# A decoder layer on one core: four of eight scatter DMAs of a group move on GpSimd, and the third state sum moves on TensorE

## Time and profile before

| | us |
|---|---|
| median of three runs | 1041.16 |
| lowest and highest run | 1039.62, 1041.73 |
| the profiled execution, its own time | 1038.75 |
| its span, first to last instruction | 1037.0 |
| TensorE busy | 905.6 (87%) |
| ScalarE busy | 725.6 (70%) |
| VectorE busy | 711.7 (69%) |
| GpSimd busy | 581.8 (56%) |
| mean granted TensorE clock | 0.962 of 2.4 GHz |

### The profile page before, as it was taken

One profiled execution on the slowest core, in us unless ns is written; L12 is line 12 of the kernel. 1 busy time (PEld: TensorE's weight loads), 2 busy tenths in 40 slices (PEclk: granted clock), 3 DMA queues, 4 the chain that ended last, 5 costly groups with the idle time before them and its releaser, 6 DMA issues.

```text
span 1037.0 us, 29540 instructions
## 1 busy us (share of the span) xinstructions
PE 905.6 (87%) x10235; PEld 579.7 (56%) x10236; DVE 711.7 (69%) x1456; ACT 725.6 (70%) x2225; POOL 581.8 (56%) x387
## 2 busy tenths in 40 slices
PE   6699899999899798989989977986955999999997
PEld 2344554554355355435534543543435999999982
DVE  1487688787678777767867767797654666666647
ACT  3587997886798698679858865964733555555556
POOL 2598268459729945972894497288033334444420
PEclk9899999999999999999999988998976999999999
DMA  4526105200700430070043006002132111111144
GB/s 122 114 52 144 32 3 115 60 11 14 164 12 21 93 84 11 15 163 12 21 97 71 11 15 143 2 20 100 67 111 60 47 48 48 46 48 47 47 120 154
DMA packets 68475, 66.63 MB, mean 64 GB/s; under 512 B 8912, under 2 KB 62352, under 8 KB 67984
## 3 DMA queue, kind: packets, MB, share of 16 engines
q1 hardware_dynamic: 63440, 55.58, 21.7%
q0 software_dynamic: 4352, 8.99, 2.6%
q10 hardware_dynamic: 576, 0.62, 0.2%
HBM read 49.03 MB, written 16.13 MB: 63 GB/s over the span
## 4 chain that ended last, share of the span: by engine, by line
PE 45%; issue 20%; POOL 13%; ACT 10%; DVE 10%; DMA 2%; SPq 0%; POOLq 0%; DVEq 0%; ACTq 0%
PE pair_a L1702 6%; PE pair_b L1706 6%; ACT prob L696 6%; POOL xg L530 4%; POOL prob L498 4%; PE y_ps L1422 3%; PE bank L1714 3%; PE y_ps L1714 3%; PE pair_b L1502 3%; PE y_ps L1502 2%; PE bank L1513 2%; POOL hst L498 2%; DVE prob L934 2%; PE pair_a L1534 2%; PE bank L1326 1%
## 5 line engine op out<-in xcount | busy, mean ns | idle before, releaser
L655 ACT ACTIVATE decays<-w,a_neg 128x256 f32<-128x256 f32 x512 | 220.9, 511 | 48.8 <-DVE prob L934 27.1
L498 POOL TENSOR_TENSOR hst<-hst,c_rep 128x1024 f32<-128x1024 f32 x64 | 151.4, 2372 | 16.5 <-DVE hst L934 15.7
L569 POOL DMA_INDIRECT y<-aoT,dest x72 | 81.3, 1129 | 132.2 <-DVE aoT L1248 128.6
L498 POOL TENSOR_TENSOR prob<-prob,c_rep 128x1024 f32<-128x1024 f32 x56 | 132.4, 2369 | 6.6 <-DVE prob L934 5.7
L530 POOL DMA_INDIRECT xg<-x_all,pos x64 | 65.6, 1025 | 92.0 <-DVE pos L1084 80.8
L934 DVE TENSOR_TENSOR_SCAN prob<-decays,pair_b 128x1024 f32<-128x1024 f32 x32 | 73.1, 2285 | 46.8 <-issue 27.6
L1422 PE MATMUL y_ps<-hst,sum 128*32 128x256 f32 x512 | 71.6, 429 | 30.4 <-POOL prob L498 30.4
L696 ACT ACTIVATE prob<-pair_b,nmax 128x128 f32<-128x128 f32 x256 | 90.4, 401 | 5.0 <-DVE nmax L992 5.0
L696 ACT ACTIVATE prob<-y_ps,nmax 128x128 f32<-128x128 f32 x256 | 90.8, 415 | 0.0
L490 POOL TENSOR_TENSOR w<-diag,b_tok 128x1024 f32<-128x1024 f32 x32 | 61.7, 1959 | 46.7 <-DVE prob L939 23.3
L1702 PE MATMUL pair_a<-qk,u 128*128 128x128 f32 x592 | 79.1, 277 | 0.0
(11 more groups left out here) (287 smaller groups left out, 2154.2 us busy)
## 6 DMA issues: line engine op xcount, KB each, us to landing
w<-d_dram SPq DMA_DIRECT2D x64, 256.0 KB, 7.0
c_rep<-c_dram SPq DMA_DIRECT2D x64, 128.0 KB, 4.0
qk<-xg SPq DMA_DIRECT2D x79, 65.0 KB
d_dram<-zpos SPq DMA_DIRECT2D x8, 512.0 KB, 3.2
xn<-in_x SPq DMA_DIRECT2D x8, 256.0 KB, 3.1
cn<-in_ctx SPq DMA_DIRECT2D x8, 256.0 KB, 3.4
mask_b<-in_mask SPq DMA_DIRECT2D x8, 256.0 KB, 3.2
w<-in_w1T SPq DMA_DIRECT2D x1, 2048.0 KB, 7.6
```

Of the source, the lines that this page charges most:

```text
L498: g_.tensor_tensor(by_state(ring(k)), by_state(ring(k)), c_rep[:, :, toks[r]].rearrange("p q (i t) -> p i q t", i=2), ALU.mult).then_inc(s ...
L569: pool.indirect_dma_start(y2[:, :], bass.IndirectOffsetOnAxis(ap=dest[:, b:b + 1], axis=0), ys[:, b % 4, :], None).then_inc(s[f"y_out{b % ...
L655: last = A(by_state(decays[:, k % 2, :])[:, :, q, :], delta_rep[:, b, toks[r]].rearrange("p (i t) -> p i t", i=2), ACT.Exp, scale=a_neg[:, ...
```

## The change

In GpSimd's block four of the eight scatters of group m-2 stay before the products of units 0 to 3; the other four go, one each, behind the first and the second `diagonals`, behind `add_q` and behind `add_bo`. In TensorE's block sum 2 moves from `k == 13` to `k == 14`, so that it stands behind `res(c, 1)` and `entries(m, 15)`, and `x1_t(g, 0)` moves up to stand directly before it. In ScalarE's block `res_out(c, 1)` and `x1_in(g, 0)` go ahead of the first `own_k`, and the four `own_k` stand together. Nothing that is computed changes.

```diff
@@ GpSimd
                 for k in range(NU - 1):
-                    if m >= 2 and k < 2 * S:
+                    if m >= 2 and k < S:
                         scatter(m - 2, (k,))
                     times_c(m, k)
...
                 if e is not None:
                     at(pool, "hc_last", m + 1)
                     diagonals(e, 0)
+                if m >= 2:
+                    scatter(m - 2, (S,))
+                if e is not None:
                     diagonals(e, 1)
+                if m >= 2:
+                    scatter(m - 2, (S + 1,))
                 add_q(m, 1)
+                if m >= 2:
+                    scatter(m - 2, (S + 2,))
                 add_bo(m)
+                if m >= 2:
+                    scatter(m - 2, (S + 3,))
@@ ScalarE
-                own_k(g, 0)
-                own_k(g, 1)
                 if c is not None:
                     res_out(c, 1)
-                own_k(g, 2)
                 x1_in(g, 0)
-                own_k(g, 3)
+                for j in range(4):
+                    own_k(g, j)
@@ TensorE
                     if k + 1 < NU and (k > 1 or not m):
                         entries(m, k + 1)
-                    if k in (9, 13):
-                        y_add(m, k // 4 - 1)
+                    if k == 9:
+                        y_add(m, 1)
+                    if k == 14:
+                        x1_t(g, 0)
+                        y_add(m, 2)
...
-                    if k == 14:
-                        x1_t(g, 0)
                     if k == 15:
                         queries(g, 0)
```

## The result

The changed kernel takes 1009.82 us (median of four runs, 1009.31 to 1011.26) beside 1040.47 us of the kernel before on the same chip: ratio 0.9707, 95% interval 0.969 to 0.9724. The profiled execution takes 1011.26 us.

The account below looks back on a forecast made before the run. Taken as the bound: TensorE's sums waiting for GpSimd products delayed by scatters. Gains 18.3 (groups 2 to 5) - 0.8 (groups 0, 1) + 8.2 + 8.2 (groups 6, 7) = 33.9 us, from 1041.16 to 1007.3 us; range 1002.5 to 1018.

Parts of the forecast that it names:

- What bounds the unit stretches: From unit 2's scan to L662, TensorE's sums wait 30.4 us for GpSimd's products, delayed by scatters; attention stays at 33.30 us.
- Part 1: Four scatters leave the unit stretch: products from unit 7 on 4.8 us earlier, groups 2 to 5 at 52.84 us.
- Part 2: Sum 2 behind entries of unit 15: `own_k` 2.8 us later, a loss of 0.4 us in each of groups 0 to 5.
- Group 6: Unit stretch: sum 1 starts earlier at full clock, GpSimd's last product ends at 630.3, then sum 3; gain 8.2 us.
- Rival (b): VectorE and GpSimd block each other on SBUF ports in group 6: 1.2 us lost, 1008.5 us; chance 0.12.
- rival (c): Groups 6 and 7 gain only the scatters' 4.8 us each, another wait taking over: 1013.9 us; chance 0.06.
- Group 7: Unit stretch: scan 11 starts 5.7 us earlier, scores give 1.0 us and sum 3 1.45 us; gain 8.2 us.
- Part 3: Four scatters in the attention stretch, around `add_q` and before `mask_bias`, fit into idle time and cost nothing.
- Rival (a): TensorE's clock falls behind its new wait for `res_out(c, 0)` in groups 0 to 5: 1017.5 us; chance 0.14.
- (d): TensorE isn't really held by GpSimd; only sum 2 moved back counts, every group loses 0.4 us: 1044.4 us; chance 0.04.
- (e): Waits of sums 1 and 2 go, but 5 us per group return in attention behind two scatters: 1041.2 us; chance 0.02.

Follow-up runs that it names:

- the scatters alone: Changed kernel with ScalarE's and TensorE's order put back, so only the four scatters move: 1010.34 us, ratio 0.9703.
- the order alone: Kernel before with only the change of ScalarE's and TensorE's order, all eight scatters staying between the products: 1036.92 us, ratio 0.996.
- keeping TensorE warm: Changed kernel plus four extra 128x128 matmuls ahead of the entries of units 12 to 15, groups 6 and 7: 1011.13 us, ratio 0.9723.
- the kernel with the fills: Only the four scatters moved, plus ten write-only GpSimd memsets beside `add_q` and `last_times_c` in groups 1 to 5: 1009.8 us.
- the guard: All eight scatters moved, old order, plus GpSimd's product of unit 0 waiting for `pos` from group 2 on: 1004.61 us, ratio 0.9676.
- the additions: Only the four scatters moved, plus four GpSimd adds reading SBUF beside `add_q` and `last_times_c` in groups 1 to 5: 1014.5 us.

## Why the prediction was right

Predicted 1007.3 us, measured 1009.82; the gain was to be 33.9 us and was 30.7. By its own steps:

- **What bounds the unit stretches.** Right, and shown from both sides: with the scatters alone, groups 2 to 5 take group 1's time within 0.04 us; with the order alone, sum 1 still waits. One number was read too smoothly: attention was not 33.30 to 33.31 us in all of groups 1 to 6 before; behind group 3 it was 33.52.
- **Part 1, groups 2 to 5**: gain 18.3 us predicted, 18.4 in the trace. The clock, at 0.97 in three of the four before, is at 1.00 in all.
- **Part 2**: 0.4 us a group predicted. 0.42 in groups 1 to 5, 0.19 in group 0. `own_k` moved by 3.1 us (2.8 predicted; its terms add up to 178.66 and not 178.5, so to 2.95), and 1.27 us of idle time before the layer norm took up the rest, as worked out.
- **Group 6**: 8.2 us predicted, 6.7 found. GpSimd's last product ended where the prediction had it (42.5 us into the stretch, 42.7 predicted). Sum 3 started 44.5 us in and not 42.8. Rival (b), at a chance of 0.12, is what happened, at about its price: `add_q` was held by the product, so that `last_times_c` started only behind it. The forecast had named the rule and yet put it at nothing in the sum. Another term stayed unnamed: with the scatters alone, group 6 gains 4.7 us, which is rival (c)'s price, since sum 2 waits 4.96 us ahead of the entries of unit 15. The way "from there as before" needed the new order, which the sum priced for groups 0 to 5 only.
- **Group 7**: 8.2 us predicted, 7.2 found. Sum 1 and scan 11 came as predicted (scan 11 at 680.94, 25.05 us in; 25.3 predicted). The missing microsecond is in "scores take 1.1 us at full clock and give 1.0 us more": they do, but start late, because TensorE is at half clock just before. In the new order sum 2 takes 2.65 us, and the scores wait 1.35 us for `own_k` behind it; keeping TensorE warm gives 0.9 us back. The order is hardly to blame: with the scatters alone, where `own_k` is done before, the queries are slow instead (1.98 us; 1.13 with TensorE warm), and the group takes 47.51 us. That the scores and sum 3 ran at full clock was in part luck: in the kernel with the fills, with the same code there as with the scatters alone, they took 2.08 and 2.94 us, and group 7 49.10.
- **Part 3**: right for these four scatters. That it would go on being right for eight was my expectation of two experiments, and wrong by 34 us.
- **Rival (a)** is refuted: TensorE waits 1.28 us for `res_out`, and the clock stays at 1.00 in groups 1 to 5 (in group 0 it is 0.98, and 0.97 before). **(c)** as a whole falls, for groups 6 and 7 gained 6.7 and 7.2 us. **(d)** and **(e)** fall with the kernel that has the scatters alone: sum 2's wait is gone from groups 2 to 5 in the old order too, and attention stays at 33.27 to 33.49 us.

The two mis-sized terms, 1.5 and 1.0 us, are the whole of what the unit stretches fell short (31.7 us for 33.9; no other group is off by more than 0.2). The measured time lies nearer to rival (b)'s 1008.5 us than to the forecast's 1007.3. The last microsecond of the miss by the medians is no term of the sum: the start, attention and tail, which vary by more than that from execution to execution.

## What to carry to other kernels

Read what a queue is busy with apart from what it waits for: here four DMA issues of 1.2 us each on GpSimd were worth 3.8 to 7.4 us a group because they stood in front of products that TensorE waited for, and nothing 20 us later on the same queue. Before an instruction is taken out of a queue, ask which wait goes with it: the scatters' wait for `pos` kept GpSimd's first product off VectorE's small instructions, and cost 1.8 us a group when it went. And repeat a gain on a second chip before you build on it: all eight scatters moved gave 3% on one chip, and a kernel that differs from it only by the guard, which explains a third of the difference, gave 0.2% on another.

## What the runs showed of the hardware that I had not expected

- A VectorE instruction of two SBUF inputs that met a GpSimd product waited to the end of it, and through the next one where that followed without a gap: `add_q`, 0.42 us alone, took 1.54, 1.85 and 2.95 us and ended each time 0.28 us after a product; `prk` took 2.04 for 0.22 us. With 0.08 us between GpSimd's instructions, the additions, it got in at the first boundary (0.78 us), and the addition behind `last_times_c` took 1.90 for 1.03 us. Ten fills of GpSimd beside the same instructions cost nothing.
- The scan of VectorE and the product of GpSimd run side by side without such a loss: 2.25 to 2.29 us a scan beside products of 2.35 us all through the unit stretches. Its second input lies in PSUM.
- Beside several scatters in a row, VectorE and ScalarE stalled for 0.5 to 4.4 us on a release that the trace gives as remote, in three kernels on two chips, and not in two kernels on a third that issue the same row at the same moments. No run here says why, or whether it is the chip.
